# Four banks for the front's x blocks, nine late scan states turned by TensorE and scaled by ScalarE, and other banks and due steps for side work

## What is computed

```python
def _mamba(x, in_w, conv_w, conv_b, xproj_w, dt_w, dt_b, A_log, D, out_w):
    xi, z = jnp.split(jnp.einsum('bld,ed->ble', x, in_w), 2, axis=-1)
    xi = jax.nn.silu(_dw_conv(xi, conv_w, conv_b))
    xdb = jnp.einsum('bld,ed->ble', xi, xproj_w)
    dtr, Bm, Cm = (xdb[..., :DTR], xdb[..., DTR:DTR + DS], xdb[..., DTR + DS:])
    dt = jax.nn.softplus(jnp.einsum('blr,dr->bld', dtr, dt_w) + dt_b)
    # scan over l:  h = exp(dt * A) * h + (dt * x) * B ;  y = sum over s of h * C
    y = _selective_scan(xi, dt, Bm, Cm, -jnp.exp(A_log), D)
    return jnp.einsum('bld,ed->ble', y * jax.nn.silu(z), out_w)

h = gelu(img_patches @ w_in.T + b_in)
r = _mamba(h, forward weights) + flip(_mamba(flip(h), backward weights)) + h
```

## Time and profile before

| | us |
|---|---|
| median of 3 timed runs | 930.74 (930.12 to 931.51) |
| the profiled execution | 922.39 |
| its span, first to last instruction | 920.7 |
| mamba front, 362.20 to 417.58 | 55.38 |
| segment 0, 417.58 to 528.50 | 110.92 |
| segment 1, 528.50 to 634.00 | 105.50 |
| segment 2, 634.00 to 739.60 | 105.60 |
| segment 3, 739.60 to 842.20 | 102.60 |
| the rest, 842.20 to 920.70 | 78.50 |

### The profile page before, as it was taken

One profiled execution on the slowest core, in us unless ns is written; L12 is line 12 of the kernel. 1 busy time (PEld: TensorE's weight loads), 2 busy tenths in 40 slices (PEclk: granted clock), 3 DMA queues, 4 the chain that ended last, 5 costly groups with the idle time before them and its releaser, 6 DMA issues. The chain is left out here.

```text
span 920.7 us, 13477 instructions
## 1 busy us (share of the span) xinstructions
PE 759.4 (82%) x3802; PEld 492.4 (53%) x3802; DVE 762.6 (83%) x1261; ACT 541.6 (59%) x1303; POOL 658.8 (72%) x454
## 2 busy tenths in 40 slices
PE   4889977899999994797879579787879766877998
PEld 2466654466666662344555455445645554422786
DVE  3588867678889985848989999999999999999843
ACT  1588855444444442476777887677775785652332
POOL 3177853477777883229999989999999999995000
PEclk9899999799999998898989799999999988799999
DMA  4000008599879844414565565656557665552001
GB/s 117 1 1 1 0 1 336 216 414 328 300 275 355 298 146 154 128 47 134 156 169 185 160 153 152 190 158 175 142 163 192 155 173 155 164 157 58 1 1 46
DMA packets 67347, 141.77 MB, mean 154 GB/s; under 512 B 12688, under 2 KB 23312, under 8 KB 65104
## 3 DMA queue, kind: packets, MB, share of 16 engines
q1 hardware_dynamic: 56432, 117.62, 42.2%
q0 software_dynamic: 6048, 18.59, 5.7%
q10 hardware_dynamic: 4800, 4.78, 1.6%
HBM read 129.92 MB, written 11.04 MB: 153 GB/s over the span
## 5 line engine op out<-in xcount | busy, mean ns | idle before, releaser
L2119 POOL TENSOR_TENSOR uB<-u,rows_B 128x1024 f32<-128x1024 f32 x127 | 297.9, 2354 | 0.0
L2339 DVE TENSOR_TENSOR_SCAN da<-da,uB 128x512 f32<-128x512 f32 x145 | 175.1, 1220 | 11.8 <-ACT da L2223 9.9
L2364 PE MATMUL ya<-ident,hV 128*128 128x128 f32 x560 | 96.2, 302 | 49.7 <-DVE hV L2238 49.6
L2129 POOL TENSOR_TENSOR hP<-hS,rows_C 128x512 f32<-128x512 f32 x96 | 121.7, 1268 | 8.3 <-PE ya L2364 3.9
L2364 PEld LDWEIGHTS ya<-ident,hV 128*128 128x128 f32 x560 | 71.4, 153 | 102.1 <-DVE hV L2238 76.3
L2336 DVE TENSOR_TENSOR_SCAN hS<-da,uB 128x512 f32<-128x512 f32 x86 | 103.6, 1204 | 6.2 <-issue 2.6
L1232 PE MATMUL gups<-wring,xT 128*128 128x448 f32 x252 | 105.8, 542 | 0.0
L1140 POOL DMA_INDIRECT xg<-x_rows,li x63 | 71.9, 1142 | 38.7 <-issue 14.6
L2238 DVE TENSOR_TENSOR hV<-da,rows_C 128x512 f32<-128x512 f32 x145 | 96.8, 668 | 0.7 <-DMA rows_C<-bc_rows 0.7
L1147 POOL DMA_INDIRECT y_rows<-y,yi x63 | 72.1, 1145 | 21.4 <-issue 17.1
L2222 ACT ACTIVATE da<-zero 128x2 f32<-128x2 f32 x145 | 25.0, 173 | 102.0 <-DVE hV L2238 101.1
(11 more groups left out here) (429 smaller groups left out, 1733.6 us busy)
## 6 DMA issues: line engine op xcount, KB each, us to landing
rows_B<-bc_rows SPq DMA_DIRECT2D x128, 256.0 KB, 3.6
rows_C<-bc_rows SPq DMA_DIRECT2D x128, 256.0 KB, 4.3
wring<-in_moe_own SPq DMA_DIRECT2D x31, 704.0 KB, 5.8
wring<-in_moe_two SPq DMA_DIRECT2D x16, 1024.0 KB, 14.3
rows_sum<-y_rows SPq DMA_DIRECT2D x6, 512.0 KB, 8.3
lut_i<-in_lut_idx SPq DMA_DIRECT2D x1, 2160.0 KB, 8.4
...
```

Of the source, the lines that this page charges most:

```text
L2119: e.tensor_tensor(uB[:, r % UPAIRS, :, :], u[:, d:d + 2, :], RB[:, r % BROWS, :].unsqueeze(1).broadcast_to([P, 2, HALF]), ALU.mult).then_i ...
L2129: e.tensor_tensor(hP[:, k % PBUF, :], hS[:, k % HBUF, :], RC[:, row % CROWS, :], ALU.mult).then_inc(s_hp, 1)
L2339: e.tensor_tensor_scan(a[:, way], a[:, way], uB[:, r % UPAIRS, b, way], 0.0, ALU.mult, ALU.add).then_inc(s_sc, 1)
L2364: mm = e.matmul(ya[n % 2][:, part], at[:, part], g.ident[:, :], start=False, stop=False, is_transpose=True, skip_group_check=True)
```

## The change

1. **Front.** x's blocks 0 to 3 get a bank each, S0, S1, ya0 and ya1, and the waits for the copies go. PE does all four after hl is done, then turns the other half's features, and each `inputs(1, m)` follows `rows(m)`. The silu table comes ahead of take(1), gelu's behind the silus. The gate's first two blocks move behind the dt matmuls, in the order 2, 3, 0, 1, and the silu of blocks 0 and 1 joins that of step 33. DVE does `low(0)` ahead of `statistics(1)`. The high parts of half 1 are copied by DVE. The decay rates of the first direction are made behind the low-rank copy, those of the second at step 9.
2. **Banks.** Segment 1's gate uses banks S0, S0, S2, S0 in place of S0, S1, S2, S0, with other due numbers, so S1 is free as fourth decay bank in steps 29 to 34 of segment 0. In segment 3 it is that in steps 0 to 6 only.
3. **Turned states (kind A).** `KINDS` writes the kinds out. Pairs 0 to 5 have what they had (20 V, 12 P). Pair 6 has 18 V, 10 P and 4 A (steps 10, 14, 19, 25), pair 7 has 17 V, 10 P and 5 A (3, 9, 13, 19, 23). Of a kind A step DVE's scan goes to hS, PE transposes the four slices of it into S1 in the order's place of the step, ACT scales each slice by C's column (a register column of `rows_turned`) into hT three steps later, and PE adds that six steps later. For it PE turns B's and C's rows at step 62 of segment 2, and ACT keeps them.
4. **Due numbers on PE.** The side program advances by the number of the step instead of by the index in the order of adds.

```diff
-UPAIRS, CBUF, PBUF, DABUF, HBUF = 3, 4, 3, 3, 4
+UPAIRS, CBUF, PBUF, DABUF, HBUF, TBUF = 3, 4, 3, 3, 4, 2
+SCALED, ADDED = 3, 6
+KINDS = ["VPVPVPVVPVPVPVVPVPVPVVPVPVPVVVVV"] * (2 * NSEG - 2) + ["VPVPVPVVPVAVPVAVPVPAVPVPVAVPVVVV",
+                                                                "VPVAVPVPVAVPVAVPVPVAVPVAPVPVPVVV"]
...
     seg, m = divmod(n, SSTEP)
     if seg == NSEG - 1:
-        return True
-    return m == SSTEP - 1 or (seg > 0 and (m < 7 or 29 <= m < 35))
+        return m < 7
+    return m == SSTEP - 1 or 29 <= m < 35 or (seg > 0 and m < 7)
...
-        XB = [S0, S1]
+        XB = [S0, S1] + ya
...
-        GZ = [[ya[0], ya[1], da[1], da[2]], [S0, S1, S2, S0], [S2] * DB, [S2] * DB]
+        GZ = [[ya[0], ya[1], da[1], da[2]], [S0, S0, S2, S0], [S2] * DB, [S2] * DB]
...
+        def keep_rows(e):
+
+            yield 62
+            e.wait_ge(s_tb, 1)
+            e.activation(sc.bT[:, :, :].rearrange("p q s -> p (q s)"), S1[:, 0:HALF // P * 2 * DS],
+                         ACT.Copy).then_inc(s_bt, 1)
+
+        def turn_state(e, n):
...
+            for q in range(HALF // P):
+                part = slice(q * P, (q + 1) * P)
+                mm = e.transpose(S1[:, part], hS[:, k % HBUF, part], g.ident[:, :])
+            mm.then_inc(s_ht, 1)
+
+        def scale_state(e, n):
+
+            i, at = turned_steps(n), DS + n // 2 % DS
+            e.wait_ge(s_ht, i + 1)
+            if i >= TBUF:
+                e.wait_ge(s_at, i - TBUF + 1)
+            for q in range(HALF // P):
+                part = slice(q * P, (q + 1) * P)
+                a = e.activation(sc.hT[i % TBUF][:, part], S1[:, part], ACT.Identity, scale=sc.bT[:, q, at:at + 1])
+            a.then_inc(s_hs, 1)
...
-                e.activation(sz[:, 0, 2:DB, :], sz[:, 0, 2:DB, :], ACT.Silu).then_inc(s_s0, 1)
+                e.activation(sz[:, 0, :, :], sz[:, 0, :, :], ACT.Silu).then_inc(s_s0, 1)
...
                 take(0)
+                e.preload_act_table_set("silu_and_others")
                 take(1)
+                take(2)
+                silu(0)
                 features(1)
-                gelu(1, 0)
-                take(2)
-                gelu(1, 1)
                 take(3)
-                e.preload_act_table_set("silu_and_others")
-                silu(0)
                 silu(1)
...
+                low(0)
                 statistics(1)
-                low(0)
                 normal(1)
...
                 for m in range(DB):
-                    if m == 2:
-                        turn(1)
-                    if m >= 2:
-
-                        inputs(1, m - 2)
-                        e.wait_ge(s_tap, m - 1)
-                    else:
+                    if m < KC:
                         e.wait_ge(s_h, m + 1)
-                    whole(in_rows(e, 0, m, XB[m % 2], s_x))
+                    whole(in_rows(e, 0, m, XB[m], s_x))
+                turn(1)
...
                 for m in range(DB):
                     rows(m)
-                e.wait_ge(s_h, KC * NH)
+                    if m < KC:
+                        inputs(1, m)
...
-                        side.advance(pair % 2 * PSTEP + i + AHEAD)
+                        side.advance((n + (0 if not late else LATE if on_pool(n) else ADDED)) % SSTEP + AHEAD)
```

More of the change, by code:

```diff
@@ L1305, in finish, with kind, turned, turned_steps @@
         self.advance(NEVER - 1)
+def kind(n):
+    return KINDS[n // PSTEP][n % PSTEP]
 def on_pool(n):
-    return n % PSTEP % 7 in (1, 3, 5) and n % PSTEP < PSTEP - LATE
+    return kind(n) == "P"
+def turned(n):
+    return kind(n) == "A"
 def pool_steps(n):
-    full, part = divmod(n, PSTEP)
-    return full * sum(on_pool(i) for i in range(PSTEP)) + sum(on_pool(i) for i in range(part))
+    return sum(on_pool(i) for i in range(n))
+def turned_steps(n):
+    return sum(turned(i) for i in range(n))
+def kept_steps(n):
+    return pool_steps(n) + turned_steps(n)
 def vector_steps(n):
-    return n - pool_steps(n)
+    return n - kept_steps(n)
+KEPT = [n for n in range(STEPS) if kind(n) != "V"]
+TURNED = [n for n in range(STEPS) if turned(n)]
 def place(n):
@@ L1356, in summed @@
 def summed(pair):
-    order = []
-    for n in range(pair * PSTEP, (pair + 1) * PSTEP):
-        if not on_pool(n):
-            order.append(n)
-        if n - LATE >= pair * PSTEP and on_pool(n - LATE):
-            order.append(n - LATE)
+    first, order = pair * PSTEP, []
+    for n in range(first, first + PSTEP + LATE):
+        if n < first + PSTEP and not on_pool(n):
+            order.append((n, False))
+        if n - LATE >= first and on_pool(n - LATE):
+            order.append((n - LATE, True))
+        if n - ADDED >= first and turned(n - ADDED):
+            order.append((n - ADDED, True))
     return order
@@ L1833, in first_dt_scalar, with first_z_scalar @@
             keep_dt(e, 0, 0)
+        def first_z_scalar(e):
+            for m in range(2):
+                yield 1 + m
+                copy_z(e, 0, m)
         def project_scalar(e, k):
@@ L1878, in first_gate_scalar @@
         def first_gate_scalar(e):
-            for due, m in ((31, 0), (35, 1), (39, 2), (41, 3)):
+            for due, m in ((27, 0), (31, 1), (36, 2), (38, 3)):
                 yield due
@@ L2227, in _ @@
                     side.advance(n % SSTEP)
+                    if n >= SCALED and turned(n - SCALED):
+                        scale_state(e, n - SCALED)
                 side.finish()
@@ L2340, in _ @@
                                              ALU.mult, ALU.add).then_inc(s_sc, 1)
-                    if n and not on_pool(n - 1):
+                    if n and kind(n - 1) == "V":
                         product(n - 1)
@@ L2437, in _ @@
                     begun = 0
-                    for i, n in enumerate(summed(pair)):
+                    for n, late in summed(pair):
                         if n % 2 == begun and begun < 2:
@@ L2442, in _ @@
                             begun += 1
-                        if on_pool(n):
+                        if turned(n) and not late:
+                            turn_state(e, n)
+                        elif turned(n):
+                            k = turned_steps(n)
+                            e.wait_ge(s_hs, k + 1)
+                            add(n, sc.hT[k % TBUF][:, :], s_at, True)
+                        elif on_pool(n):
                             k = pool_steps(n)
```

116 lines of the change are left out of this document (75 added, 41 removed).

## The result

The changed kernel takes 950.31 us (949.27 to 952.62, 4 runs) where the kernel before takes 930.43: a ratio of 1.0217 (95% interval 1.0195 to 1.024), 20 us slower. The forecast was 932.0 in a range of 925.5 to 935.5, so the size was wrong by a factor of fifteen and the time lies outside the range.

What follows compares the result with a forecast made beforehand. It took POOL and DVE in turns as the bound in the segments, and one chain through all engines in the front. -2.4 - 1.4 + 2.4 + 2.7 = +1.3 on profiled 922.4 gave 932.0 us timed, range 925.5 to 935.5.

Steps and rivals of the forecast that it cites:

- Item 1: Front: waits for x's shared banks go and PE's rows start earlier, so the first scan comes earlier, -2.4 us.
- Item 2: Step 33 of segment 0: a fourth decay bank cuts DVE's wait for decay 34 from 3.75 to 2.4, -1.4 us.
- Item 3: Segments 0 to 2: PE's side work comes due earlier, ahead of adds that POOL waits for, +2.4 us.
- item a: Step 62 of segment 2: ACT keeps the turned rows ahead of decay 63, so scan 2 comes later, +1.6 us.
- what absorbs: -1.4: Part of Item 3: POOL's waits for DVE and slack at segment 3's start take back 1.4 of 3.8 us.
- Item 4: Segment 3: nine turned states save DVE and POOL products but add waits, +2.7 us in sum.
- b: Step 14 of segment 3: scaling of state 10 waits for its turn on PE, making decay 14 late, +1.5 us.
- c: Into pair 7: a late add and an hP stand on PE ahead of the turned sums; gates follow 1.6 us later.
- d: Step 39 of segment 3: the turn of state 35 stands behind skips and adds; decay 39 is 1.4 us late.
- (e): Segment 3: the other seven scalings on ACT, each 1.27 us in front of a decay, cost 0.6 us.
- -4.0 in throughput: Segment 3: the gain from taking 5 products off DVE and 4 off POOL, -4.0 us.
- The rival R2: Heads of segments 1 and 2: PE at its lower clock level, +3.4 us, 935.4 us; chance 0.18.

Runs made afterwards that it cites:

- e5: The changed kernel with only its front left: old kinds, old PE due numbers, gate in its old banks with old due numbers; ratio 0.9993 to the kernel before.
- e6: e3 with ACT's four copies of segment 1's gate blocks, and PE's due numbers for them, moved later; ratio 1.0014 to the kernel before.
- e10: e6 with extra PE passes before the first projection, the fourth gate block earlier on PE and its copy one step later; 926.19 us, ratio 0.9955.
- e4: The kernel before with one line changed: PE's side program advances by the step number; ratio 1.0076.
- e2: The changed kernel with no turned states or kept rows and segment 3's fourth bank back; ratio 1.0101 to the kernel before.
- e3: The changed kernel with the edits of e1 and e2 together, so only front and bank changes are left; ratio 1.0036 to the kernel before.
- e1: The changed kernel with PE's side program advancing by the index in the order of adds again; ratio 1.0171 to the kernel before.
- e13: e10 with eight turned states placed to avoid the measured waits; ratio 0.9957 to the kernel before.

## Why the prediction was wrong

**Item 1, front (-2.4, measured -0.9).** The order and the places were right: rows(0) came 37.1 us behind the last y_rows, which is my 393.9. The step that failed is "PE does 4 x 2.04 of rows and 2 x 1.72 of inputs", priced at the full clock. In this order PE idles 2.04 us ahead of rows(0), and the rows behind it ran at 0.61, which costs 1.65. The rest of the item holds: from rows(0) to the first scan I had 21.3 us (393.9 to 415.2), and it is 21.06 in every profile at 1.00. The fronts at 1.00 are 2.5 to 4.2 us shorter than before's 60.8; that spread lies ahead of rows(0).

**Item 2, step 34 (-1.4, measured +3.8 for the segment).** The wait itself came to 2.89, my first estimate of 2.9 and not the 2.36 that I took; e5's 0.85 confirms the grown block. The step that failed is a term that is missing: the change also puts ACT's four copies of the gate blocks 3 to 4 steps earlier, and I costed that at nothing without a word. They stand in front of decays 28 and 39 (and 32 with the old due numbers) and wait for PE: 2.65 + 2.22 = 4.9 us. e6 and e10 show that moving them gives it back.

**Item 3, due numbers (+2.4, measured +2.7 in segment 1, +3.2 with item a in segment 2, and +7.0 for all in e4).** Counted by scans, the first pair of segment 1 lost 1.4 (steps 16 to 24), my price, and POOL waited 2.87 for my 2.8. That hit is part luck: the four passes took 0.83 longer than at full clock, and in segment 2, where they had it, POOL waited 0.96 and the first pair lost nothing. In e4, where the clock was 0.72 there (652 to 656), it lost 1.4 again. Two terms failed. "About as long as the add is early there: +0.1" for the second pairs: at steps 54 and 56 they lost 1.3 in segment 1 and 2.7 in segment 2. PE stood there for dtr, 2.84 and 2.61 us, and POOL behind it 1.21 and 2.40. The wait is worth 1.2 to 1.3 (segment 1, and segment 2 in e2 and e4, all with the clock at 1.00 behind it), and the clock of 0.58 behind it the other 1.4. I had compared lengths of products with the slack and not asked what they wait for. And "what absorbs: -1.4": nothing did. In e4 segments 1 and 2 each end 2.9 late, and segment 3 adds 0.7 where I had counted on it to give back.

**Item 4, turned states (+2.7, measured +9.3 and +1.1 in the tail).** Against e3, the scans of the changed kernel fall behind as follows: 1.6 by step 4 (item a: 1.6), 2.2 at step 14 (b: 1.5), 4.5 up to step 24 (not foreseen), 1.2 up to step 28 (not foreseen; DVE waits 1.11 for uB there, and POOL before that 7.1 for an add), 1.4 at the gates (c: 1.6), 1.7 at step 39 (d: 1.4). So (a) to (d) are there, in size partly by luck: with the old due numbers (e1) (a) costs 3.2 and the gates 3.4. The step that failed is (e), "0.6 for the other seven scalings", priced by their length alone. One of them, of state 19, stands on ACT ahead of decay 23 and waits for its turn 5.37 us. Item 3 meets item 4 there: PE reaches the dt product so early that it waits 3.73 for ACT's copy of dt, with 5.8 us of adds, products and then that turn queued behind. With either part alone this wait isn't there (e1, e2). Yet by stage the two together cost only 2.1 more than apart (9.3 against e1's 6.9 and e2's 0.3), since e1 loses more at its output product and its gates. The other failed term is "-4.0 in throughput": behind step 39 the turned kernel wins back 2.4, in e13 2.7. That a product less on DVE saves its 0.585 only where no wait holds DVE is how I read it; no run isolates it.

**For item 4 I took the upper end of my own bounds, and that was still too low.** The rival R2 had a true mechanism, which explains 0.8 of the first wait in segment 1 and, at a place that it didn't name, 1.4 of segment 2. It was far too small. No rival had one engine's wait for a second hold up work that a third instruction, on that second engine, then waits for.
